# First batch of an attention and expert block: GpSimd's products to VectorE, its convolution adds to a tree of adding DMAs, and identity turns of TensorE moved ahead of the next batch's x

## The chip, the cores and the metric

One core of a Trainium2 chip runs the whole kernel. The metric is device time in microseconds, from the start to the end of one execution, as the median of several runs. Beside it stands one profiled execution, whose trace gives the start and the length of every instruction. The engines are TensorE (PE), VectorE (DVE), ScalarE (ACT), GpSimd (POOL) and SyncE (SP), which here only issues DMAs.

## The reference

The input is x of 4 batches, 1024 positions and 128 channels, float32. Two residual blocks follow each other; the first is the one that matters here.

```python
x = x + _layernorm(_L0_attn_ref(_layernorm(x), Wqkv, Wo, conv_w))
x = x + _layernorm(_L0_ffn_ref(_layernorm(x), gate_W, W1, b1, W2, b2, Ws1, bs1, Ws2, bs2, route_scale))

# inside the attention, 8 heads of 16 channels, offsets 0, 1, 2, 4, ... 512
sc = einsum('bhsd,bhskd->bhsk', qh, kg) / sqrt(d)      # q times k, k taken offset positions back
w = softmax(where(valid, sc, -inf))
tele = einsum('bhsk,bhskd->bhsd', w, vg)               # weighted v, offset positions back
conv = causal depthwise convolution of v with 7 taps
low = fq @ (fk.T @ v) / (fq . sum(fk) + 1e-6)          # fq, fk = elu + 1
return x + (tele + conv + low) @ Wo
```

The second block is a mixture of eight experts (two taken per position by a sigmoid gate) with a shared one. It starts one batch behind the attention, so that the first batch's attention runs alone.

## The kernel before

Everything is held in on-chip memory. A batch is 8 tiles of 128 positions (NT), two halves of 512 columns. The loop over b runs five times: in turn b the attention of batch b and the experts of batch b - 1 (units u0 and u1, its halves) are written into the same five instruction streams, one function for each engine. Each engine executes its stream in the order in which it stands; semaphores tie the streams together. Nothing reorders them, so a wait holds up all that stands behind it on its engine.

The attention of one batch goes like this. `product(eng, s, q)` (L283 is its multiply) multiplies qT with kT shifted by an offset, both channel-major, 1024 columns at a time (512 for the offset 512 and, in the first batch, in the first of three groups `s`). There are 4, 4 and 3 of them in the groups 0, 1 and 2; `sum_heads(b, s)` on TensorE (L1324) sums each head's channels into psA. A group's products lie in one of two sets of buffers, so that the third group waits for the sum of the first. Beside it VectorE makes the features fkT (L943) and fqT (L948), and TensorE makes the state kv (L1303), which VectorE masks (L974). After the third group the scores are copied by ScalarE, turned by TensorE, and VectorE does the softmax on them (`softmax_logits` from L982 on, `softmax_weights`), with the exponentials on ScalarE (L692). `weigh(b, j)` (L1026) then multiplies, tile by tile, the values v_tok and their shifted copies v_shift with the weights, into a ring of four buffers (TERM_BUFS); `sum_terms(b, j)` (L1353, L1356) on TensorE sums a tile's terms. Behind tile 4 stands `add_conv(b, 0)` (L1046), which adds the convolution's first half, and behind tile 7 `add_conv(b, 1)`. TensorE's sum of tile 4 and all behind it wait for the first of these, since the bank is used again. v_shift is made by 20-odd DMAs that SyncE issues as soon as v_tok is there.

The convolution is a sum of 7 taps. ScalarE scales each (`scale_first_taps`, L625: taps 0 to 3 behind fk_tok, taps 4 to 6 behind the scores) into buffers named by `first_tap(tap)`: convT, three tapT, gate_shared, x3T and hid. In the later batches six accumulating DMAs that GpSimd issues (`add_tap`, L495) sum them. In the first batch GpSimd itself does, by twelve adds of 512 columns (`first_conv`, L459), the first half ahead of the second. GpSimd also does three of the first batch's eleven products, those in POOL_PRODUCTS. Its stream in the first batch is: constants, the three products, gate_constants (three affine selects, L466), ln1 of the next batch (L489 to L492), the twelve adds, ln2 of the first half.

TensorE makes identity turns that nobody reads in three places of the first batch: WARM_UP at the start, FIRST_FILL_SUM (20) ahead of the third group's sum, FIRST_FILL_TERMS (24) behind the next batch's k and q projections and ahead of the first `sum_terms` (`keep_busy`, L1468). The next batch's x is normalised by ScalarE (`normalise1`, L598) behind the exponentials and when ln1 is done, and turned by TensorE (`turn_x`, L1252).

## Time and profile before

| | us |
|---|---|
| median of 3 runs | 300.31 (300.30 to 300.32) |
| the profiled execution, whole | 298.65 |
| its span, first to last instruction | 296.9 |
| busy in the span: TensorE, VectorE, ScalarE, GpSimd | 250.2, 245.5, 198.4, 110.9 |

The span is what the trace's times are counted in. The median lies 3.4 us above it. The page's chain of waits is the work that ended last, followed back from the end; a row of it says from when on and for how long the end waited for which operation. In a timeline row the numbers are start and length in microseconds, and the bracket tells how long the engine sat idle before it and which operation released it; where instructions are merged, the length is that of all. In a row by form the numbers behind the bar are busy time in microseconds, the mean in nanoseconds, and the idle time before. L numbers are lines of the kernel before.

### The profile page before, as it was taken

How to read it: one execution, taken by the hardware profiler on the slowest of the kernel's cores; microseconds unless marked ns; L12 is line 12 of the kernel's file. 1: busy time of each engine (PE TensorE's matmuls, PEld its weight loads, DVE VectorE, ACT ScalarE, POOL GpSimd, SP SyncE). 2: the span in 40 equal slices, each digit the busy share in tenths (PEclk: the TensorE clock that was granted, in tenths of full speed). 3: DMA queues.
4: the chain of work that ended last, by engine and by line, in shares of the span. 5: the costliest groups of instructions: out<-in, count | busy, mean ns of one | idle time of the engine just before them, and what ended most of it. 6: DMA issues, size and time to landing. Idle time of an engine off the chain costs nothing.

```text
span 296.9 us, 4788 instructions
## 1 busy us (share of the span) xinstructions
PE 250.2 (84%) x1639; PEld 173.5 (58%) x1639; DVE 245.5 (83%) x570; ACT 198.4 (67%) x461; POOL 110.9 (37%) x161
## 2 busy tenths in 40 slices
PE   5849909887699899989898899989898697699893
PEld 5424605776165467678546486777555485584383
DVE  6699989988997699799896899799957997727743
ACT  3476655447879956898499746989597253476841
POOL 5967699522434004025471104046530141230023
PEclk9998977999799999999999999999999999999999
DMA  7527602003989730308999601019899301000003
GB/s 202 129 78 216 195 0 72 2 0 62 235 244 202 172 71 0 108 0 164 253 236 234 127 9 38 0 27 226 265 218 217 71 3 35 0 3 1 0 13 95
DMA packets 22963, 31.34 MB, mean 106 GB/s; under 512 B 3909, under 2 KB 17054, under 8 KB 22938
## 3 DMA queue, kind: packets, MB, share of 16 engines
q1 hardware_dynamic: 20346, 21.59, 25.6%
q0 software_dynamic: 2592, 9.44, 17.5%
q8 instruction: 13, 0.21, 0.3%
q14 instruction: 12, 0.10, 0.1%
HBM read 5.07 MB, written 2.10 MB: 24 GB/s over the span
## 4 chain that ended last, share of the span: by engine, by line
PE 41%; DVE 31%; ACT 18%; issue 5%; POOL 4%; POOLq 0%; DVEq 0%; ACTq 0%
DVE prods L1026 7%; DVE prods L283 5%; PE psH L1356 5%; PE psY L1459 4%; PE psF L1421 3%; PE psG L1459 3%; PE psA L1459 3%; PE psA L1252 3%; DVE hid L1137 3%; PE psA L1324 2%; ACT xn L718 2%; PE psF L1396 2%; ACT xn L598 2%; DVE den L997 2%; PE psY L1303 2%
## 5 line engine op out<-in xcount | busy, mean ns | idle before, releaser
L474 POOL TENSOR_SCALAR var<-ss 128x4 f32<-128x4 f32 (+1 forms) x25 | 13.5, 539 | 105.8 <-ACT squares L764 51.6
L283 DVE TENSOR_TENSOR prods<-qT,kT 128x1024 f32<-128x1024 f32 (+1 forms) x44 | 50.9, 1212 | 2.2 <-ACT qT L587 2.2
L1356 PE MATMUL psH<-ident,prods 128*128 128x128 f32 x324 | 40.1, 273 | 0.0
L1356 PEld LDWEIGHTS psH<-ident,prods 128*128 128x128 f32 x324 | 36.4, 141 | 2.3 <-issue 2.3
L1026 DVE TENSOR_TENSOR prods<-v_shift,prob 128x896 f32<-128x896 f32 x32 | 35.7, 1115 | 0.0
L1137 DVE TENSOR_TENSOR hid<-hid,psG 128x512 f32<-128x512 f32 x32 | 20.8, 683 | 15.8 <-PE psG L1445 15.2
L476 POOL TENSOR_TENSOR rstd<-var,neg_half 128x4 f32<-128x4 f32 (+2 forms) x28 | 31.8, 1137 | 2.3
L1324 PE MATMUL psA<-prods,slot_sel 128*32 128x512 f32 x168 | 26.1, 677 | 6.1 <-DVE prods L283 5.9
L1421 PE MATMUL psF<-x3T,w 128*128 128x512 f32 x58 | 29.0, 610 | 0.4 <-ACT gexp L732 0.3
L1026 DVE TENSOR_TENSOR prods<-v_tok,prob 128x128 f32<-128x128 f32 (+2 forms) x60 | 25.5, 450 | 0.0
L495 POOL DMA_DIRECT2D convT<-tapT x9 | 8.2, 913 | 43.4 <-DMA convT<-tapT 24.6
L1260 PE MATMUL psA<-xnT,wqkv 128*128 128x512 f32 x36 | 18.6, 646 | 1.6 <-ACT xnT L587 1.6
L1459 PE MATMUL psY<-w,hid 128*128 128x128 f32 x140 | 16.6, 277 | 3.2 <-DVE prods L1010 3.2
L1459 PEld LDWEIGHTS psY<-w,hid 128*128 128x128 f32 x140 | 15.9, 192 | 5.7 <-DVE prods L1010 5.7
L740 ACT ACTIVATE hid<-psF,b1c 128x512 f32<-128x512 f32 x29 | 18.6, 682 | 0.7 <-PE psF L1421 0.5
L1421 PEld LDWEIGHTS psF<-x3T,w 128*128 128x128 f32 x58 | 9.7, 189 | 12.5 <-issue 8.5
L1468 PE MATMUL psG<-ident 128*128 128x128 f32 x100 | 14.0, 302 | 3.1 <-POOL ident L409 3.1
L1468 PEld LDWEIGHTS psG<-ident 128*128 128x128 f32 x100 | 13.1, 158 | 5.2 <-POOL ident L409 3.1
L1324 PEld LDWEIGHTS psA<-prods,slot_sel 128*32 128x32 f32 x168 | 5.5, 115 | 15.8 <-issue 13.5
L1353 PE MATMUL psH<-ident,prods 128*128 128x128 f32 x32 | 9.2, 288 | 6.2 <-DVE prods L1046 3.9
L764 ACT ACTIVATE squares<-psY 128x128 f32<-128x128 f32 x14 | 3.7, 277 | 14.8 <-PE psY L1459 14.8
L660 ACT ACTIVATE tapT<-vT,cw 128x1024 f32<-128x1024 f32 x12 | 13.1, 1137 | 0.0
(237 smaller groups left out, 612.1 us busy)
## 6 DMA issues: line engine op xcount, KB each, us to landing
v_shift<-v_tok SPq DMA_DIRECT2D x20, 448.0 KB
convT<-tapT POOLq DMA_DIRECT2D x9, 512.0 KB, 4.9
x_res<-L_attn_x SPq DMA_DIRECT2D x4, 512.0 KB, 9.6
out<-y_out SPq DMA_DIRECT2D x7, 256.0 KB, 2.3
x_in<-L_attn_x SPq DMA_DIRECT2D x3, 512.0 KB, 4.1
v_shift<-v_tok SPq DMA_DIRECT2D x4, 384.0 KB
tapT<-tapT POOLq DMA_DIRECT2D x3, 512.0 KB, 9.8
convT<-kexp POOLq DMA_DIRECT2D x3, 512.0 KB, 7.5
```

Source lines behind the costliest of these rows:

```text
L283: return eng.tensor_tensor(prods[:, QUADS * (s % 2) + q, t0:t1], qT[:, t0:t1], kT[:, PRE - off + t0:PRE - off + t1], ALU.mult)
L474: nc.gpsimd.tensor_scalar(var[:, cols], src, scale, EPS, ALU.mult, ALU.add).then_inc(step, 1)
L476: return nc.gpsimd.tensor_tensor(rstd[:, cols], var[:, cols], neg_half[:, cols], ALU.pow)
L740: nc.scalar.activation(hid[:, c, half_cols(u)], hidden_bank(u, c), ACT.Gelu, bias=b1c[:, c:c + 1]).then_inc(hidden_free, 1)
L1026: return nc.vector.tensor_tensor(dst, src.rearrange("p m (h d) -> p m h d", d=HD), w, ALU.mult)
L1137: nc.vector.tensor_tensor(hid[:, c, cols], hid[:, c, cols], psG[:, c % 2, :], ALU.mult).then_inc(gated, 1)
L1260: pe.matmul(psA[:, half, :], wqkv[:, bass.ts(part, P)], xnT[(b + 1) % 2][:, bass.ts(half, HALF)], start=True, stop=True).then_inc(psA_full, 1)
L1324: ins = pe.matmul(psA[32 * q:32 * q + 32, half, :], ksum_sel[:] if low else slot_sel[:, s, :], fqT[:, cols] if low else prods[:, QUADS * ( ...
L1356: ins = pe.matmul(dst, terms[:, j % TERM_BUFS, m, :], ident[:], is_transpose=True, start=False, stop=(m == live[-1]))
L1421: pe.matmul(hidden_bank(u, c), w1[:, bass.ts(c, P)], x3T[:, half_cols(u)], start=True, stop=True).then_inc(hidden_full, 1)
L1459: ins = pe.matmul(output_tile(u, n), hid[:, c, bass.ts(j, P)], w2[:, c, :], start=(c == CH - 1), stop=(c == CH - 2))
L1468: pe.transpose(bank[:, bass.ts(k % TPH, P)], ident[:], ident[:])
```

## The change

Three things, all in the first batch. First, POOL_PRODUCTS and `first_pool_products` go: VectorE does all eleven products. Second, `first_conv` goes: six accumulating DMAs of 512 KB, issued by GpSimd, sum the seven taps as a tree, 1 into 0, 3 into 2 and 5 into 4, then 2 into 0 and 6 into 4, then 4 into 0. The first three are issued ahead of ln1 of the next batch, the other three behind it; each waits for the taps and for the DMAs that it builds on. Both halves' `add_conv`, and the first tap of the next batch, wait for the last DMA. Third, 40 identity turns (FIRST_FILL_X) stand ahead of the next batch's `turn_x`, and FIRST_FILL_TERMS is 10 in place of 24.

GpSimd's stream before, from the last constants to the first adds (line numbers differ between the two kernels by a few; gate_sel is the constant of gate_constants, L489 to L492 are ln1):

```order
L442 MEMSET neg_half 1x1
L283 TENSOR_TENSOR prods<-qT,kT 128x1024 x3
L466 AFFINE_SELECT gate_sel<-gate_sel 24x512 x3
L470 MEMSET neg_half 1x1
L489 TENSOR_SCALAR neg_mean<-mv 128x8
L474 TENSOR_SCALAR var<-mv 128x8
L476 TENSOR_TENSOR rstd<-var,neg_half 128x8
L492 TENSOR_TENSOR nmr<-neg_mean,rstd 128x8
L459 TENSOR_TENSOR convT<-convT,tapT 128x512 x3
```

And the same place after the change:

```order
L442 MEMSET neg_half 1x1
L469 AFFINE_SELECT gate_sel<-gate_sel 24x512 x3
L473 MEMSET neg_half 1x1
L445 DMA convT<-tapT 128x1024
L445 DMA tapT<-tapT 128x1024
L445 DMA gate_shared<-x3T 128x1024
L492 TENSOR_SCALAR neg_mean<-mv 128x8
L477 TENSOR_SCALAR var<-mv 128x8
L479 TENSOR_TENSOR rstd<-var,neg_half 128x8
L495 TENSOR_TENSOR nmr<-neg_mean,rstd 128x8
L445 DMA convT<-tapT 128x1024
L445 DMA gate_shared<-hid 128x1024
```

The products and the adds are gone, the selects have moved up, and ln1 now stands behind the first three DMAs.

TensorE's stream before, from the turned scores to the first term sum:

```order
L1252 MATMUL psA<-ident,prods 128x128 x8
L1342 MATMUL psH<-kv,fqT 128x128 x4
L1342 MATMUL psY<-kv,fqT 128x128 x4
L1252 MATMUL psA<-ident,xn 128x128 x8
L1260 MATMUL psA<-xnT,wqkv 128x512 x4
L1468 MATMUL psG<-ident 128x128 x24
L1353 MATMUL psH<-ident,prods 128x128
```

And after:

```order
L1254 MATMUL psA<-ident,prods 128x128 x8
L1342 MATMUL psH<-kv,fqT 128x128 x4
L1342 MATMUL psY<-kv,fqT 128x128 x4
L1468 MATMUL psG<-ident 128x128 x40
L1254 MATMUL psA<-ident,xn 128x128 x8
L1262 MATMUL psA<-xnT,wqkv 128x512 x4
L1468 MATMUL psG<-ident 128x128 x10
L1353 MATMUL psH<-ident,prods 128x128
```

A row of 40 turns stands ahead of the turning of xn, and the row behind the projections is shorter by 14.

```diff
--- before.py
+++ after.py
@@ -47,8 +47,7 @@
 SLOTS, QUADS = 3, 4
 TERM_BUFS = 4
 WARM_UP = 20
-FIRST_FILL_SUM, FIRST_FILL_TERMS = 20, 24
-POOL_PRODUCTS = ((0, 3), (1, 3), (2, 2))
+FIRST_FILL_SUM, FIRST_FILL_X, FIRST_FILL_TERMS = 20, 40, 10
 FILL_SUM = 12
 FILL_FRONT = 5
 FILL_X3, FILL_C4, FILL_LOGITS = 10, 4, 8
@@ -243,7 +242,8 @@
         terms_ready, terms_summed = sem("terms_ready"), sem("terms_summed")
         tap_scaled, sums_added, side_added = sem("tap_scaled"), sem("sums_added"), sem("side_added")
         first_ld, first_xn = [sem(f"first_ld{h}") for h in range(2)], [sem(f"first_xn{h}") for h in range(2)]
-        first_turned, first_products, first_taps, first_added = sem("first_turned"), sem("first_products"), sem("first_taps"), sem("first_added")
+        first_turned, first_taps = sem("first_turned"), sem("first_taps")
+        first_pairs, first_sums = [sem(f"first_pair{i}") for i in range(3)], [sem(f"first_sum{i}") for i in range(3)]
         hT_ready, y_ready = sem("hT_ready"), sem("y_ready")
         ss2_ready, x2_ready, ss3_ready, xn3_ready = sem("ss2_ready"), sem("x2_ready"), sem("ss3_ready"), sem("xn3_ready")
         front_full, front_free = sem("front_full"), sem("front_free")
@@ -441,23 +441,26 @@
                     nc.gpsimd.memset(first_pref[:, :, e:e + 1], float(EXPERTS - e))
                 nc.gpsimd.memset(neg_half[0:1, 0:1], -0.5).then_inc(consts_ready, 1)
 
-            def first_pool_products():
-                pool.wait_ge(consts_ready, 2)
-                pool.wait_ge(psA_free, freed(-1, PSA_Q, 1))
-                for s, q in POOL_PRODUCTS:
-                    if s == 2:
-                        pool.wait_ge(group_summed, 1)
-                    product(nc.gpsimd, s, q).then_inc(first_products, 1)
-
-            def first_conv(half):
-
-                cols = bass.ts(half, HALF)
-                for tap in range(1, TAPS):
-                    pool.wait_ge(first_taps, tap + 1)
-                    if tap > 1:
-                        pool.wait_ge(first_added, (TAPS - 1) * half + tap - 1)
-                    nc.gpsimd.tensor_tensor(convT[0][:, cols], convT[0][:, cols], first_tap(tap)[:, cols],
-                                            ALU.add).then_inc(first_added, 1)
+            def add_first(into, tap, signal):
+                nc.gpsimd.dma_start(first_tap(into), first_tap(tap), accum_op=ALU.add).then_inc(signal, N_DMA)
+
+            def first_conv_pairs():
+                for pair in range(2):
+                    pool.wait_ge(first_taps, 2 * pair + 2)
+                    add_first(2 * pair, 2 * pair + 1, first_pairs[pair])
+                pool.wait_ge(first_taps, 6)
+                add_first(4, 5, first_pairs[2])
+
+            def first_conv_sums():
+                pool.wait_ge(first_pairs[0], N_DMA)
+                pool.wait_ge(first_pairs[1], N_DMA)
+                add_first(0, 2, first_sums[0])
+                pool.wait_ge(first_taps, TAPS)
+                pool.wait_ge(first_pairs[2], N_DMA)
+                add_first(4, 6, first_sums[1])
+                pool.wait_ge(first_sums[0], N_DMA)
+                pool.wait_ge(first_sums[1], N_DMA)
+                add_first(0, 4, first_sums[2])
 
             def gate_constants():
                 for part in range(3):
@@ -545,8 +548,8 @@
             first_rstds()
             constants()
             more_constants()
-            first_pool_products()
             gate_constants()
+            first_conv_pairs()
             for b in range(B + 1):
                 attn, ffn, more = b < B, b >= 1, b < B - 1
                 u0, u1 = 2 * b - 2, 2 * b - 1
@@ -566,8 +569,7 @@
                     ln4(u0)
                     add_residual(u0)
                 if b == 0:
-                    first_conv(0)
-                    first_conv(1)
+                    first_conv_sums()
                 if attn:
                     ln2(2 * b)
                 if more:
@@ -648,7 +650,7 @@
                     if tap == 0:
                         act.wait_ge(psA_free, freed(b - 1, PSA_V, 1))
                         if b == 1:
-                            act.wait_ge(first_added, 2 * (TAPS - 1))
+                            act.wait_ge(first_sums[2], N_DMA)
                         else:
                             act.wait_ge(hT_ready, upto(b - 1, 2, 0))
                     elif tap == 4:
@@ -955,7 +957,7 @@
                     dve.wait_ge(y_ready, upto(b, 2, 0))
                 if s == 2:
                     dve.wait_ge(group_summed, upto(b, 2, 1))
-                mine = [q for q in range(QUADS) if TERMS[SLOTS * q + s] != LOW and (b or (s, q) not in POOL_PRODUCTS)]
+                mine = [q for q in range(QUADS) if TERMS[SLOTS * q + s] != LOW]
                 if b == 0 and s == 0:
                     dve.wait_ge(psA_free, first_count(PSA_Q, 0))
                     for q in mine:
@@ -963,7 +965,7 @@
                     dve.wait_ge(psA_free, first_count(PSA_Q, 1))
                 for n, q in enumerate(mine):
                     ins = product(nc.vector, s, q, HALF if b == 0 and s == 0 else 0, T)
-                    ins.then_inc(prod_ready, 2 if b == 0 and q == mine[-1] else 1)
+                    ins.then_inc(prod_ready, 1)
                     beside(n)
 
             def linear_state(b, beside):
@@ -1041,7 +1043,7 @@
                 if b:
                     dve.wait_ge(sums_added, N_DMA * upto(b - 1, N_SUMS, N_SUMS))
                 else:
-                    dve.wait_ge(first_added, (TAPS - 1) * (half + 1))
+                    dve.wait_ge(first_sums[2], N_DMA)
                 cols = bass.ts(half, HALF)
                 nc.vector.tensor_tensor(hT[:, cols], psH[:], convT[b % 2][:, cols], ALU.add).then_inc(hT_ready, 1)
 
@@ -1306,8 +1308,6 @@
             def sum_heads(b, s):
 
                 pe.wait_ge(prod_ready, upto(b, N_PRODUCTS[2], N_PRODUCTS[s]))
-                if b == 0:
-                    pe.wait_ge(first_products, s + 1)
                 if s == 2:
                     pe.wait_ge(fq_ready, upto(b, 1, 1))
                     pe.wait_ge(kv_ready, upto(b, 1, 1))
@@ -1506,6 +1506,8 @@
                     if ffn:
                         turn_x3(u1)
                         gates_expert_major(u0)
+                    if b == 0:
+                        keep_busy(FIRST_FILL_X, psG[:, 1, :])
                     if more:
                         turn_x(b + 1)
                     if ffn:
```

## Rows read from the trace of the kernel before

**Rows 1.** Chain of waits: start us, us, what; first batch.

```profile
...
12.43 10.91 DVE prods L283 x9
...
31.53 0.18 DVE kv L974
...
36.24 0.13 DVE zden L982
...
46.64 7.85 DVE prods L1026 x7
...
59.81 0.61 DVE prods L1046
...
60.85 1.20 PE psH L1356 x11
...
69.07 0.70 DVE prods L1046
...
```

**Rows 2.** VectorE's groups by form, 75 to 240 us: shapes, busy us, mean ns, idle.

```profile
...
L283 DVE TENSOR_TENSOR prods<-qT,kT 128x1024 f32<-128x1024 f32 x27 | 31.5, 1213 | 0.0
L1026 DVE TENSOR_TENSOR prods<-v_shift,prob 128x896 f32<-128x896 f32 x19 | 20.6, 1083 | 0.0
...
L1026 DVE TENSOR_TENSOR prods<-v_tok,prob 128x128 f32<-128x128 f32 x22 | 6.3, 284 | 0.0
...
L283 DVE TENSOR_TENSOR prods<-qT,kT 128x512 f32<-128x512 f32 x3 | 2.0, 668 | 0.0
...
```

**Rows 3.** Groups by form, VectorE, 12 to 31 us.

```profile
...
L283 DVE TENSOR_TENSOR prods<-qT,kT 128x512 f32<-128x512 f32 x7 | 8.6, 1303 | 2.2 <-ACT qT L587 2.2
L283 DVE TENSOR_TENSOR prods<-qT,kT 128x1024 f32<-128x1024 f32 x4 | 5.6, 1445 | 0.0
...
```

**Rows 4.** Timeline, TensorE: start us, us, instructions, idle before and releaser.

```profile
...
29.30 2.35 PE L1468 MATMUL psG<-ident 128*128 128x128 f32 x20
...
44.03 1.30 PE L1252 MATMUL psA<-ident,xn 128*128 128x128 f32 x5 [7.09 <-ACT xn L598]
...
```

**Rows 5.** Timeline, ScalarE and GpSimd, 27 to 41 us.

```profile
...
27.24 3.24 ACT L625 ACTIVATE tapT<-vT,cw 128x1024 f32<-128x1024 f32 x3
...
34.04 0.20 POOL L489 TENSOR_SCALAR neg_mean<-mv 128x8 f32<-128x8 f32 x1 [2.39 <-DVE mv L921]
...
35.38 1.14 ACT L625 ACTIVATE x3T<-vT,cw 128x1024 f32<-128x1024 f32 x1
...
36.31 0.20 POOL L492 TENSOR_TENSOR nmr<-neg_mean,rstd 128x8 f32<-128x8 f32 x1
...
40.76 3.18 ACT L598 ACTIVATE xn<-x_in,nmr,rstd 128x128 f32<-128x128 f32 x8
...
```

**Rows 6.** Windows: PE, PEld, DVE, ACT, POOL busy, TensorE clock, DMA share, GB/s.

```profile
...
41.50:44.00 2.50, 0.00 (x0) 0.00 (x0) 2.43 (x3) 2.43 (x7) 2.27 (x2) 0.50 0.00 0
44.00:48.00 4.00, 3.97 (x11) 2.73 (x12) 3.93 (x6) 1.28 (x3) 3.80 (x3) 0.50 0.45 131
...
```

**Rows 7.** Accumulating DMAs: issues, landings at 71, 134, 103; windows; v_shift's queue.

```profile
...
70.37 1.11 POOL L495 DMA_DIRECT2D convT<-tapT  x1 [3.78 <-ACT tapT L660]
71.16 1.21 POOL L495 DMA_DIRECT2D tapT<-tapT  x1
...
convT<-tapT POOLq DMA_DIRECT2D x1, 512.0 KB, 4.8
tapT<-tapT POOLq DMA_DIRECT2D x1, 512.0 KB, 9.2
...
tapT<-tapT POOLq DMA_DIRECT2D x1, 512.0 KB, 11.0
...
convT<-tapT POOLq DMA_DIRECT2D x1, 512.0 KB, 4.5
...
104.00:108.00 4.00, 3.78 (x9) 1.52 (x10) 3.86 (x8) 2.98 (x5) 0.17 (x1) 1.00 0.69 131
...
q1 hardware_dynamic: 102, 0.27, 49.3%
...
```

## The prediction

> **What bounds the kernel now.** I read the chain of waits first, since it says whose work sets the end, and only its first 70 us, since the change touches nothing behind them. In the first batch the chain is VectorE's nearly all the way: it starts the products at 12.4 us, reads the turned scores at 36.24, starts to weigh the values at 46.64, adds the first half's convolution at 59.81 and the second half's at 69.07 [rows 1]. Next I ask which of these steps are as long as they have to be. The same operations have undisturbed durations in the later batches, where GpSimd adds and multiplies nothing: a product of 1024 columns 1213 ns, of 512 columns 668 ns, a v_shift term 1083 ns, a v_tok term of one tile 284 ns [rows 2]. In the first batch the same two products take 1445 and 1303 ns [rows 3]; the difference falls together with GpSimd's own three products and its adds. TensorE is the second reader: its identity fill of 2.35 us ends just as kv is ready (31.7), it then waits 7.09 us for the next batch's xn, and works on at half clock behind that [rows 4, 6]. ScalarE, GpSimd's order and the DMAs come last, because they are what the change leans on [rows 5, 7].
>
> **Part 1, products on VectorE.** VectorE gets nine products of 512 and six of 1024 columns instead of seven and four. The first two groups have nine of 512 and three of 1024: 9 x 0.668 + 3 x 1.213 = 9.7 us by the undisturbed durations (less by what overlaps between neighbours), against the 10.91 us that seven and two take now beside GpSimd [rows 1 to 3]. GpSimd's three affine selects of gate_sel, which ran behind its products, now run beside these; VectorE's last two products lay beside them at 1445 ns or so against 1213, so three selects may cost some 0.7 to 1.4 us. I take the keys' features 0.6 us earlier (bounds: 0.5 later to 1.5 earlier). Here TensorE takes over: it turns fk, sums the second group, makes kv's sum, and then has 20 identity turns of 2.35 us before the third sum. In the profile that fill is just covered by VectorE; now VectorE is earlier, so the fill is on the path, and the third sum comes only 0.6 to 0.7 us earlier. The turned scores are then complete at about 34.5, where VectorE, which comes from kv to zden in 4.5 us (31.7 to 36.24 [rows 1]), would be there at 33.7 and waits. So the softmax starts at 34.5 for 36.24: **1.7 us**.
>
> **Part 2, no adds on GpSimd.** The twelve adds of 512 columns go. They run beside the softmax and the first tiles. VectorE weighs tiles 0 to 4 in 59.81 - 46.64 = 13.2 us. The same fourteen terms undisturbed are 5 x 1.083 + 6 x 0.284 + three of two or three tiles, each under 0.6 (at most 384 of a v_shift term's 896 columns): 8.2 to 8.9 us [rows 1, 2]. With the softmax's own multiply undisturbed as well, weighing would start at 44.0 and reach the first convolution add at 51.7 to 52.9.
>
> **Part 3, the 40 turns.** They fill the 7.09 us of TensorE's wait. 20 turns take 2.35 us in the profile [rows 4], so 40 take 4.7: from about 36.2 to 40.9, before xn is there (42.4, below), so they delay nothing. TensorE's clock stands at 0.50, its 1.2 GHz level, from the end of that wait until 48 [rows 6]; kept at 2.4 GHz the turns of xn and the four projections no longer lag, and with 10 turns for 24 the first term sum can start at about 48.4 (ScalarE empties xnT, kT and qT in six steps from 43.0 on). A tile's sum is 11 turns in 1.20 us [rows 1], four tiles of 9 to 11 turns under 4.6: TensorE has tiles 0 to 3 at 52.9. So by the engines alone the first add would come at **52.9**, 6.9 us early.
>
> **Part 4, ln1 behind three DMAs.** GpSimd computes neg_mean to nmr of the next batch from 34.04 to 36.51 [rows 5]; the change puts the wait for tap 5 ahead of it. ScalarE writes tap 5 (x3T) from 35.38 to 36.5 [rows 5], 0.7 earlier with the scores: 35.8. An issue of 0.8 us and ln1's 2.5 us follow: 39.2. ScalarE's xn waits for that, but also for its own exponentials, behind which it starts at 40.76 now [rows 5] and at 39.1 then. A tie: it costs 0.1 to 0.2, xn is done at 42.4.
>
> **Part 5, the tree of DMAs.** It is new work for the DMA engines, and the convolution add of VectorE waits for its root. Six accumulating DMAs of 512 KB, three levels deep, on one queue. The rows: such a DMA with nothing beside it lands 4.5 us after its issue, of which its data keep the DMA engines busy for 0.69 of 4 us, about 2.8 us; of two issued 0.8 us apart beside v_shift's traffic the first lands after 4.8, the second after 9.2, which is 71.16 + 9.2 - 70.37 - 4.8 = 5.2 us behind the first; a second one at 134 us landed after 11.0 [rows 7]. Here v_shift runs until 36 (the last 49% slice [rows 7]) and, with two accumulations beside it, until about 41, still ahead of its reader at 45. The sum: tap 1 is written at 28.3 [rows 5], now 27.9; first pair lands after some 7 (between 4.8 and the pair's shared 9.2): 34.9; second 5.2 behind it: 40.1; third, issued at 35.9, 3.8 behind it (between 2.8 and 5.2, since v_shift ends there): 43.9; the add of 2 into 0, queued at 40.2, shares the DMA engines with the next x load, 4.0: 47.9; the add of 6 into 4, issued at 44.0, 2.8 behind it: 50.7; only then the last, 4.5: **55.2**. VectorE adds at 55.3 or 55.4. Bounds: with 4.8 for the first and 2.8 for each queued one (the third is issued at 35.9 and takes 4.5) the root lands at about 50.5; with 11.0 - 4.8 = 6.2 or 5.2 for each it lands at 62. Both ends are kept. I take 55.4 since both kinds of rows, shared and alone, occur on its way.
>
> The Trainium skill ("DMA: Bandwidth & Descriptors", the SWDGE path) gives about 2.0 us plus bytes / 436 GB/s for a DMA issued by GpSimd, 3.2 us here and 1.2 for a queued one; the profile's rows have 4.5 and 2.8 [rows 7], so accumulation is dearer than that fit. By the fit the tree would be done before 50 and the add would come at 52.9.
>
> **Behind the add** nothing is changed: from the first convolution add to the second 69.07 - 59.81 = 9.3 us, mostly TensorE (tile 4's sum, the output, the projection of v, three sums). But TensorE now sits idle from 52.9 until 56.1, and the profile shows what it does after idle: 0.50 behind the 7.09 us wait [rows 4, 6]. With a shorter wait it may fall or not; if it does, some 2.4 us of turns at 1.2 GHz cost 1.2 us. I count it.
>
> **The sum.** First add 59.7 -> 55.4: -4.3; clock +1.2: -3.1. Against the profiled execution: span 296.9 -> 293.8. The median of the runs stands 3.4 above that span (300.31), with the same distance 297.2.
>
> **Rivals.** (A) *The tree is no bound*: it lands before 52.9, VectorE never waits, the whole 6.8 us come: 293.5. For it: 2.8 us of data per DMA, and half of the tree behind v_shift's traffic. Against: depth three with 4.5 at its end, one queue. (B) *The tree lands later than GpSimd's adds did*. With 5.2 for every queued one and 6 for the second, as when v_shift or x traffic is beside all of them, the root is at 61 to 62; VectorE, TensorE and the next batch stand behind the add; TensorE is idle for over 8 us and starts at 1.2 GHz for 3 to 4 us of work, +1.7. The time is 300.3 + (61.3 - 59.7) + 1.7 = 303.6. It decides at a root at 58.0: from there on the saving no longer pays for the clock. For it: both ends of the rows reach it, and nothing in the profile shows an accumulation issued beside another queue's backlog of this size in the first batch. (C) *They cancel*: root at 57.7 to 58.3, 300.3. (D) *The change does not do what it says*: VectorE's products were not slowed by GpSimd but by something in batch 0 alone, so the scores come 0.5 late, the terms stay slow and the first add comes at about 59: within 0.5 us of now. Rows 2 against 3 speak against it, since only what lies beside GpSimd's work is slow.
>
> **How the numbers follow.** Tree as bound, add between 53.6 and 57.7 (forecast 297.2, its own range 295.2 to 299.5): 0.52. A: 0.20. B: 0.17. C and D: 0.11, of which about 0.08 within 0.2% (0.6 us, about what a measurement of this kernel can tell from no change), the rest a little faster or slower. Faster 0.73, same 0.08, slower 0.19. The range reaches from A's time less half a us, 293.0, to 301.5, which leaves out the worse half of B and little below: about 0.1 each side.
>
> **What would show it.** In the changed profile: products of 512 and 1024 columns near 668 and 1213 ns but for the three selects; kv and the scores under 1 us earlier, zden at 34.5 behind TensorE; ln1's nmr near 39.2 and xn done at 42.4; clock 1.00 through 41 to 48; v_shift terms at 1083 ns; VectorE idle ahead of its first convolution add for 2 to 4 us, released by a DMA, at 55.4; a stretch of 0.50 behind it; 9.3 to 10.5 us to the second add. It is wrong if VectorE does not wait there (A), if it waits until after 58 (B), if v_shift lands after 45, or if a later batch loses what the first gains.

## The result, and the profile after

The changed kernel takes 297.75 us at the median (295.9 to 300.19, 17 runs), the kernel before 300.31 beside it. The ratio is 0.992 with a 95% interval of 0.9901 to 0.9938: 2.4 us faster, 1.9 to 3.0. The forecast was 297.2. Its profiled execution has a span of 295.5 us, for 296.9 before, which is only 1.4. Executions of one and the same kernel here spread over 4 us (298.87 to 303.25 before), and the longer ones mostly have the lower mean granted clock of TensorE (in the changed kernel 0.957 at 300.19 and 0.984 at 295.9, though 0.979 at 299.81). So a comparison of two traces tells where time is spent, and the ratios and medians tell how much. The ratios leave out executions over 1.5% above the same kernel's shortest; the medians beside them are of all. The profiled execution of before took 298.65, below the shortest of the 17 beside it (298.87). So the pair of traces accounts for 1.4 us of the 2.4 to 2.6, and no kept trace shows where the rest lies.

The chain of waits of the changed kernel, the steps of its first batch (start us, us, what), which answer to [rows 1]:

```profile
...
12.52 10.34 DVE prods L283 x12
...
31.74 2.18 PE psG L1468 x20
...
40.28 2.28 POOL rstd L479
...
42.87 3.19 ACT xn L600 x8
...
58.28 0.70 DVE prods L1048
...
67.64 0.70 DVE prods L1048
...
```

The chain that was VectorE's has become TensorE's, GpSimd's and ScalarE's: through the fill of 20 turns, through ln1's power behind the third DMA, through xn, and then on TensorE to the first convolution add (the projections and tiles are left out of the lines above). That add is at 58.28 for 59.73, 1.45 us earlier; the second at 67.64 for 69.07, 1.43 earlier, and nothing of this is lost later (1.4 at the end). So the whole gain of this execution stands at the first add, and 9.36 us lie between the adds as before.

VectorE's groups by form from 12 to 31 us, to be read against [rows 3], and from 43 to 67 us against [rows 2]:

```profile
...
L283 DVE TENSOR_TENSOR prods<-qT,kT 128x1024 f32<-128x1024 f32 x6 | 7.0, 1215 | 0.0
L283 DVE TENSOR_TENSOR prods<-qT,kT 128x512 f32<-128x512 f32 x9 | 6.9, 840 | 2.2 <-ACT qT L589 2.2
...
```

```profile
...
L1028 DVE TENSOR_TENSOR prods<-v_shift,prob 128x896 f32<-128x896 f32 x8 | 8.7, 1085 | 0.0
L1028 DVE TENSOR_TENSOR prods<-v_tok,prob 128x128 f32<-128x128 f32 x9 | 2.5, 285 | 0.0
...
```

VectorE works undisturbed now, except for the products of 512 columns that lie beside the three selects: 840 ns for 668, 1.5 us over nine. But VectorE no longer decides. Its timeline from 31 to 59 us has the waits:

```profile
...
31.77 0.29 DVE L976 TENSOR_TENSOR kv<-psY,head_mask 128x128 f32<-128x128 f32 x1 [3.08 <-PE psY L1305]
...
37.26 0.23 DVE L984 TENSOR_SCALAR zden<-psA 128x64 f32<-128x64 f32 x1 [0.67 <-PE psA L1254]
...
58.28 0.69 DVE L1048 TENSOR_TENSOR prods<-psH,convT 128x512 f32<-128x512 f32 x1 [1.73 <-PE psH L1356]
...
```

kv is no earlier than before (31.77 for 31.44), and VectorE reads the turned scores 1.1 us later (37.26 for 36.16). On TensorE they are complete 2.0 us later, at 37.1 for 35.1; before, VectorE came to them last. The windows of the same trace (busy time of PE, PEld, DVE, ACT, POOL, then TensorE's granted clock, DMA share, GB/s) show why:

```profile
...
20.00:22.00 2.00, 1.97 (x12) 0.24 (x4) 2.00 (x3) 0.57 (x1) 0.00 (x0) 0.50 0.85 245
22.00:24.00 2.00, 0.00 (x0) 0.00 (x0) 2.00 (x4) 0.00 (x0) 0.00 (x0) 0.50 0.85 253
24.00:29.00 5.00, 4.94 (x22) 2.16 (x22) 4.70 (x6) 3.53 (x5) 0.00 (x0) 0.50 0.77 234
...
47.00:50.00 3.00, 2.87 (x5) 1.18 (x4) 3.00 (x7) 1.39 (x3) 0.00 (x0) 0.50 1.07 179
...
```

TensorE runs at 0.50, its 1.2 GHz level, from 19.7 to 29.9 us. It had been idle from 16.5 to 18.95, summed the first group, and was idle again from 22 to 24 for the keys' features. The turns of fk, the second group and kv's sum, which took from 24.5 to 29.3 before, take from 24.1 to 31.6. The turns of fk, before and after:

```profile
...
24.54 1.09 PE L1252 MATMUL psF<-ident,fkT 128*128 128x128 f32 x8 [0.67 <-DVE fkT L943]
...
```

```profile
...
24.06 1.97 PE L1254 MATMUL psF<-ident,fkT 128*128 128x128 f32 x8 [2.09 <-DVE fkT L945]
...
```

How long the clock is down here differs between executions. Five kernels of the experiments below (products only, no tree, ln1 first, and the two with the root on VectorE and no early fills) give TensorE the same work up to this place. In their traces the clock is up until 24 to 25 us and down only from there to about 28; kv is ready at 30.6 to 30.9 and zden starts at 36.1 to 36.4. The old fills have it as here (31.87 and 37.35). So some 1 us of what is late in this trace is this execution's, and two traces are fairly compared only when their clocks fall in the same places.

A second such place lies in the next batch. From the second convolution add of the first batch to the first one of the second batch it is 51.4 us in the traces of before, changed, products only, no tree, early fills, ln1 first and the two last kernels, where the clock is back by about 79 us. It is 52.8 to 53.1 in old fills, early fills and a hold, fills only, tree only and the root alone, and 54.3 in the one without the fill of 20, where it is down later, beside more of TensorE's work. The same windows of the changed kernel, then of the old fills:

```profile
...
75.00:78.00 3.00, 2.59 (x14) 0.22 (x4) 2.96 (x19) 2.96 (x10) 2.60 (x5) 0.56 0.88 211
81.00:84.00 3.00, 3.00 (x30) 2.12 (x31) 3.00 (x8) 1.47 (x3) 0.00 (x0) 1.00 0.80 252
...
```

```profile
...
75.00:78.00 3.00, 1.92 (x16) 0.42 (x16) 3.00 (x8) 3.00 (x17) 1.45 (x2) 1.00 1.09 214
81.00:84.00 3.00, 2.47 (x5) 1.43 (x6) 3.00 (x6) 0.84 (x2) 0.00 (x0) 0.53 0.78 241
...
```

These 1.4 to 2.9 us are in the times of the experiments and not in their first batch. Most executions of the kernel before are 1.6 us longer than its profiled one, which this place could explain; it isn't shown, since only one trace of each kernel is kept.

The tree, by GpSimd's issues and the time from issue to landing, in us:

| DMA | issued | takes | landed |
|---|---|---|---|
| 1 into 0 | 29.06 | 6.8 | 35.9 |
| 3 into 2 | 31.13 | 10.5 | 41.6 |
| 5 into 4 | 38.80 | 5.4 | 44.2 |
| 2 into 0 | 43.12 | 4.8 | 47.9 |
| 6 into 4 | 44.76 | 6.9 | 51.7 |
| 4 into 0, the root | 52.16 | 4.5 | 56.7 |

```profile
...
52.16 0.85 POOL L445 DMA_DIRECT2D convT<-gate_shared  x1 [6.54 <-DMA gate_shared<-hid]
...
```

```profile
...
convT<-gate_shared POOLq DMA_DIRECT2D x1, 512.0 KB, 4.5
...
```

In this execution the tree is done 1.6 us before TensorE is.

### The profile page after: what moved, and what is told of

It is laid out like the page before. It is cut to its first block, busy times and chain, and to the rows that moved or that the text cites. A ratio compares the mean times of both kernels' runs of the same rounds, so it can differ in the third digit from the quotient of the medians.

```text
span 295.5 us, 4824 instructions
## 1 busy us (share of the span) xinstructions
PE 253.9 (86%) x1665; PEld 175.9 (60%) x1665; DVE 236.4 (80%) x574; ACT 198.6 (67%) x461; POOL 88.3 (30%) x152
## 4 chain that ended last, share of the span: by engine, by line
PE 49%; DVE 20%; ACT 20%; POOL 5%; issue 5%; POOLq 0%; DVEq 0%; ACTq 0%
PE psH L1356 6%; PE psA L1324 4%; PE psY L1459 4%; PE psA L1262 4%; DVE prods L283 3%; PE psF L1421 3%; DVE prods L1028 3%; ACT xn L600 3%; PE psG L1459 3%; PE psA L1459 3%; PE psA L1254 3%; DVE hid L1139 3%; PE psY L1305 3%; POOL rstd L479 2%; ACT xn L720 2%
## 5 line engine op out<-in xcount | busy, mean ns | idle before, releaser
L1356 PEld LDWEIGHTS psH<-ident,prods 128*128 128x128 f32 x324 | 36.4, 141 | 2.3 <-issue 2.3
L1028 DVE TENSOR_TENSOR prods<-v_shift,prob 128x896 f32<-128x896 f32 x32 | 34.7, 1083 | 0.0
L479 POOL TENSOR_TENSOR rstd<-var,neg_half 128x4 f32<-128x4 f32 (+2 forms) x28 | 32.5, 1160 | 2.3
L1324 PE MATMUL psA<-prods,slot_sel 128*32 128x512 f32 x168 | 27.4, 705 | 4.2 <-DVE prods L283 4.2
L1028 DVE TENSOR_TENSOR prods<-v_tok,prob 128x128 f32<-128x128 f32 (+2 forms) x60 | 20.8, 373 | 2.1 <-PE psH L1356 2.1
L1468 PE MATMUL psG<-ident 128*128 128x128 f32 x126 | 16.4, 289 | 3.1 <-POOL ident L409 3.1
L1468 PEld LDWEIGHTS psG<-ident 128*128 128x128 f32 x126 | 15.5, 150 | 5.2 <-POOL ident L409 3.1
L1324 PEld LDWEIGHTS psA<-prods,slot_sel 128*32 128x32 f32 x168 | 5.5, 118 | 14.5 <-issue 12.2
```

The source lines that it names most:

```text
L479: return nc.gpsimd.tensor_tensor(rstd[:, cols], var[:, cols], neg_half[:, cols], ALU.pow)
L1028: return nc.vector.tensor_tensor(dst, src.rearrange("p m (h d) -> p m h d", d=HD), w, ALU.mult)
L1324: ins = pe.matmul(psA[32 * q:32 * q + 32, half, :], ksum_sel[:] if low else slot_sel[:, s, :], fqT[:, cols] if low else prods[:, QUADS * ( ...
L1356: ins = pe.matmul(dst, terms[:, j % TERM_BUFS, m, :], ident[:], is_transpose=True, start=False, stop=(m == live[-1]))
L1468: pe.transpose(bank[:, bass.ts(k % TPH, P)], ident[:], ident[:])
```

## First experiments: the three parts alone

The experiments come in three groups; each kernel ran beside the kernel before on the same chip. The first four take the change apart.

**Products only.** GpSimd's three products go to VectorE, nothing else.

```diff
-POOL_PRODUCTS = ((0, 3), (1, 3), (2, 2))
+POOL_PRODUCTS = ()
...
-            first_pool_products()
...
-                if b == 0:
-                    pe.wait_ge(first_products, s + 1)
```

> Of the three parts only the first: VectorE makes all eleven products of the first batch; GpSimd's adds and TensorE's fills stand as in the kernel before. Theory P (what bounds the first batch after the change is TensorE up to the scores, at 1.2 GHz from 19.7 to 29.9 us, so faster products gain nothing there): kv at 31 to 32 us as before, scores not earlier, the time within 0.6 us of the kernel before (300.3), rather 0.3 to 1 slower since the fill of 20 turns is no longer covered. Rival Q (VectorE's products were the gain): 1.5 to 2.5 us faster, 298 to 299.

Measured: ratio 0.994, interval 0.991 to 0.9969, median 299.15 against 300.35. Theory P's range for the time is missed, and Q's nearly met, though the trace is nearer to P: kv is 0.75 us earlier (30.69), zden is where it was, and the first convolution add is 0.2 us earlier than before, the second too (68.87):

```profile
...
36.17 0.23 DVE L981 TENSOR_SCALAR zden<-psA 128x64 f32<-128x64 f32 x1 [0.67 <-PE psA L1251]
...
59.52 0.68 DVE L1045 TENSOR_TENSOR prods<-psH,convT 128x512 f32<-128x512 f32 x1
...
```

The two traces are 0.2 us apart in their spans too (296.7 for 296.9), the medians 1.2, the ratio 1.8 and the means of all executions only 0.6 (299.92 for 300.55). The rest lies in how the executions are spread, which a single trace doesn't show. It stays open whether the products alone gain anything.

**Fills only.**

```diff
-FIRST_FILL_SUM, FIRST_FILL_TERMS = 20, 24
+FIRST_FILL_SUM, FIRST_FILL_X, FIRST_FILL_TERMS = 20, 40, 10
...
+                    if b == 0:
+                        keep_busy(FIRST_FILL_X, psG[:, 1, :])
```

> Only the third part: 40 identity turns ahead of the next batch's x and 10 in place of 24 behind it. Theory P: the term sums of TensorE start 2 to 3 us earlier (50.5 for 53.3) but VectorE, slowed by GpSimd's adds, comes to its first convolution add at nearly the same time, so at most the 0.95 us that it stands ahead of tile 3 is gained: 299.3 to 300.3. Rival Q (the clock of TensorE behind its wait was the bound): 2 us or more faster, under 298.3.

Measured: ratio 1.0095, interval 1.0056 to 1.0134, median 304.04. A miss for both theories: the fills alone make the kernel 2.9 us slower. The trace (TensorE's timeline, then windows) shows how:

```profile
...
55.54 0.33 PE L1353 MATMUL psH<-ident,prods 128*128 128x128 f32 x1 [2.24 <-DVE prods L1026]
...
61.64 0.45 PE L1353 MATMUL psH<-ident,prods 128*128 128x128 f32 x1 [0.87 <-DVE prods L1046]
61.88 2.55 PE L1356 MATMUL psH<-ident,prods 128*128 128x128 f32 x11
...
```

```profile
...
53.00:57.00 4.00, 1.73 (x14) 1.25 (x12) 4.00 (x5) 1.71 (x2) 3.42 (x2) 1.00 0.00 0
57.50:61.00 3.50, 2.61 (x11) 2.21 (x11) 2.47 (x5) 0.00 (x0) 0.00 (x0) 0.50 0.00 0
61.00:67.00 6.00, 5.36 (x25) 5.39 (x26) 5.51 (x10) 0.00 (x0) 0.00 (x0) 0.50 0.00 0
...
```

With 10 turns for 24 TensorE comes to the term sums at 51 us, and VectorE, which GpSimd's adds slow, can't feed it: it is busy 1.73 of 4 us, the clock falls to 1.2 GHz at 57.3, and the eleven turns of a tile take 2.55 us for 1.36. The first add is at 60.81, the second 12.2 us behind it at 72.98, for 9.3; of the 5.3 us by which the span is longer, 3.9 stand there and 1.4 in the next batch. TensorE, early at a slow feeder, lost its clock here. That it need not is seen in the trace of the kernel without the tree, below.

**Tree only.** The tree stands in place of `first_conv`, GpSimd keeps its products, the fills are the old ones.

```diff
-                    first_conv(0)
-                    first_conv(1)
+                    first_conv_sums()
...
-                    dve.wait_ge(first_added, (TAPS - 1) * (half + 1))
+                    dve.wait_ge(first_sums[2], N_DMA)
```

> Only the second part: the tree of DMAs in place of GpSimd's twelve adds; GpSimd keeps its three products, the fills are as before. Theory P: scores at 36.2 as before or a little later (ln1 stands behind tap 5, so xn is later by 2 us), v_shift terms at 1.08 us, VectorE's first convolution add at 58 to 59 behind TensorE, not behind a DMA: 0.5 to 1.5 us faster, 298.8 to 299.8. Rival R (the tree is the bound): VectorE waits for a DMA ahead of that add, 300 or more.

Measured: ratio 0.9961, interval 0.9935 to 0.9987, median 299.37; P's range, 1.2 us faster. VectorE's timeline has the first add released by TensorE, so R falls; it is 1.25 us earlier than before, and 1.7 us are lost again in the next batch:

```profile
...
58.48 0.69 DVE L1058 TENSOR_TENSOR prods<-psH,convT 128x512 f32<-128x512 f32 x1 [1.73 <-PE psH L1368]
...
```

**No tree.** The changed kernel with `first_conv` back: products on VectorE, new fills, GpSimd's adds.

```diff
-                    first_conv_sums()
+                    first_conv(0)
+                    first_conv(1)
```

> Products on VectorE and the fills as in the changed kernel, but GpSimd's twelve adds in place of the tree. Theory P: the scores come 1 us later than before (the fill on TensorE's path), the terms are slowed by the adds again (v_shift and v_tok terms with means above 1.1 and 0.4 us), the first convolution add at 60 to 61: 300.3 to 301.5, so that the whole gain of the change hangs on the tree. Rival Q: under 299.

Measured: ratio 1.0012, interval 0.9972 to 1.0051, median 301.27: no gain without the tree, Q falls. The adds slow the terms as before (groups by form, 43 to 67 us; with the tree they are 1085 and 285 ns):

```profile
...
L1017 DVE TENSOR_TENSOR prods<-v_shift,prob 128x896 f32<-128x896 f32 x8 | 9.7, 1212 | 0.0
L1017 DVE TENSOR_TENSOR prods<-v_tok,prob 128x128 f32<-128x128 f32 x9 | 5.1, 580 | 0.0
...
```

Its profiled execution is one of its shortest, 298.39, and has the first add at 59.50, earlier than P said. TensorE has the same early start and the same gaps there as in fills only, and keeps its clock:

```profile
...
53.00:57.00 4.00, 1.73 (x16) 1.49 (x15) 4.00 (x6) 2.55 (x3) 2.07 (x2) 1.00 0.00 0
57.50:61.00 3.50, 2.44 (x21) 1.99 (x19) 3.50 (x8) 0.00 (x0) 0.00 (x0) 1.00 0.00 0
...
```

So the same busy time went before a fall in one trace and before none in the other. That the longer executions of this kernel (up to 303.64) are those with a fall is likely, and not shown.

The parts alone come to -0.6%, +0.95% and -0.4%, together about nothing; the whole is -0.8%. So they are not additive. The fills cost beside GpSimd's adds (0.95% here, and 0.7% from products only to no tree) and pay beside the tree (1.1% from the old fills, below, to the changed kernel). What tree and fills give with GpSimd's products kept wasn't run.

## Second group: what bounds the changed kernel

**The old fills.** The changed kernel with no turns ahead of xn and 24 behind the projections.

```diff
-FIRST_FILL_SUM, FIRST_FILL_X, FIRST_FILL_TERMS = 20, 40, 10
+FIRST_FILL_SUM, FIRST_FILL_X, FIRST_FILL_TERMS = 20, 0, 24
```

> The changed kernel with the fills of the kernel before: none ahead of the next batch's x, 24 behind its k and q projections. Theory P (the parts are worth something only together: the fills need the tree, since TensorE then reaches the term sums first and VectorE, no longer slowed by GpSimd's adds, keeps it busy): TensorE idles about 7 us ahead of xn, its projections at 1.2 GHz and 24 turns put the first term sum at 55 to 56, the first convolution add at 59.5 to 60.5: 1 to 2.5 us slower than the changed kernel, 298.8 to 300.3. Rival Q (the fills are worth nothing or harm, as they do alone): the same as the changed kernel or faster, 297.8 or less.

Measured: ratio 1.0028, interval 1.0001 to 1.0055, median 300.65: 2.9 us above the changed kernel. Direction and trace as P said, a little more than its range. TensorE's turns of xn follow an idle of 7 us, and 24 turns in place of 10 put the sums later; the first add is at 60.13 for 58.28, with the same clock ahead of the scores in both traces. That is 1.85 us of the 3.3 between the spans; the other 1.5 stand in the next batch, where the clock is down later:

```profile
...
52.84 2.78 PE L1468 MATMUL psG<-ident 128*128 128x128 f32 x24
...
```

```profile
...
60.13 0.69 DVE L1048 TENSOR_TENSOR prods<-psH,convT 128x512 f32<-128x512 f32 x1 [1.73 <-PE psH L1356]
...
```

**ln1 first.** Only the third DMA moves behind ln1.

```diff
-                pool.wait_ge(first_taps, 6)
-                add_first(4, 5, first_pairs[2])
...
             def first_conv_sums():
+                pool.wait_ge(first_taps, 6)
+                add_first(4, 5, first_pairs[2])
```

> The changed kernel with only the third DMA (tap 5 into tap 4) moved behind ln1 of the next batch on GpSimd. Theory P (behind the softmax the chain runs through tap 5, that issue, ln1 and xn to TensorE, and the tree has 1.6 us to spare at its root): nmr at 37 us for 42.8, xn starts behind the exponentials at 41.9 for 42.9, the first convolution add 0.7 to 1.2 us earlier: 296.6 to 297.1 by the median. Rival R (the tree's root is the bound, or right behind it): the third DMA is issued at 38.8 as before, nothing moves by more than 0.5 us.

Measured: ratio 0.9912, interval 0.9877 to 0.9948, median 298.28: no difference from the changed kernel that can be told, so P's gain in time is missed. In its trace ln1's last step is at 35.69, 7 us earlier, and TensorE has tiles 0 to 3 at 54.7 for 58.2. Of these 3.5 us, 1.0 is in the scores already (zden at 36.26) and 1.4 in the projections (3.80 us for 5.23), both by this execution's clock; the edit's own part is about 1.1, the wait of 0.96 for nmr that is gone. VectorE stands and waits for the tree's root:

```profile
...
57.41 0.69 DVE L1048 TENSOR_TENSOR prods<-psH,convT 128x512 f32<-128x512 f32 x1 [4.07 <-DMA convT<-gate_shared]
68.42 0.69 DVE L1048 TENSOR_TENSOR prods<-psH,convT 128x512 f32<-128x512 f32 x1 [1.85 <-PE psH L1356]
...
```

The first add gains 0.9 us, and then 11.0 us lie between the adds for 9.4, since TensorE has idled and its clock is down from 58.2 to 61.7. The two bounds, TensorE and the tree, lie 1.6 us apart in the changed kernel's trace, and in this one the clock takes back what was gained.

**No fill ahead of the third sum.**

```diff
-FIRST_FILL_SUM, FIRST_FILL_X, FIRST_FILL_TERMS = 20, 40, 10
+FIRST_FILL_SUM, FIRST_FILL_X, FIRST_FILL_TERMS = 0, 40, 10
```

> The changed kernel without the 20 identity turns ahead of the third group's sum. Theory P (that fill is on the path, 31.57 to 33.9 us in the trace of the changed kernel, where VectorE's kv is ready at 31.8): the scores and the zden step come 1.5 to 2.1 us earlier (VectorE's weight centring is then the bound at 36.4 to 36.6, so zden at 36.5 for 37.3: 0.7 us only on VectorE), xn 0.9 to 1.2 us earlier through tap 5, the first add about 1 us earlier: 296.5 to 297.2. Rival S (the fill holds the clock up): 1.2 GHz in the scores and their turning, no gain or up to 1 us slower.

Measured: ratio 1.001, interval 0.9976 to 1.0045, median 300.84: slower than the changed kernel by some 3 us, beyond what S said. Its profiled execution starts the products 1.4 us later than the others, at 13.88, behind GpSimd's last constant; counted from there, zden (at 36.67) is 0.8 us earlier than in the five traces with the same clock, which bears out P's path. But the add again waits for the root, at 58.24, and the second one follows 11.0 us later, in part at 1.2 GHz; a further 2.9 us are lost in the next batch. S's reason isn't seen: the clock is 1.00 through the scores and their turning (30 to 41 us). The profiled execution is its longest (302.04), and why most of the others are over 300 stays open.

**Early fills.** 18 turns ahead of the first group's sum, 24 behind it.

```diff
                         token_major_v(b)
                         pe.wait_ge(consts_ready, 1)
+                        keep_busy(18, psG[:, 1, :])
                     sum_heads(b, 0)
+                    if b == 0:
+                        keep_busy(24, psG[:, 1, :])
```

> The changed kernel with 18 identity turns ahead of the first group's sum and 24 behind it, in the stretches where TensorE waits for VectorE (16.5 to 18.9 and 22 to 24 us). Theory P (what was lost against the forecast is TensorE's clock, at 1.2 GHz from 19.7 to 29.9): the clock stays at 2.4 GHz, kv at 28.9 to 29.4 for 31.8, zden at 34.6 for 37.3, the first convolution add at 55.5 to 56.5: 1.8 to 2.8 us faster than the changed kernel, 295 to 296. Rival T (the turns only take TensorE's time, or the tree becomes the bound at 56.5): 0.5 us or less.

Measured: ratio 1.0004, interval 0.9963 to 1.0045, median 301.2. The time is T's and worse, the trace (298.57, one of its short executions) is P's up to the softmax. Here the clock is up from 16 to 44 us, and the turned scores are there when the forecast had them (34.5):

```profile
...
16.00:24.00 8.00, 7.13 (x62) 5.21 (x61) 8.00 (x11) 4.52 (x6) 0.56 (x2) 1.00 0.38 106
24.00:30.00 6.00, 5.98 (x50) 4.37 (x51) 5.67 (x11) 5.25 (x6) 1.11 (x1) 1.00 0.76 234
...
58.50:61.50 3.00, 2.60 (x13) 2.63 (x14) 3.00 (x7) 0.00 (x0) 0.00 (x0) 0.50 0.00 0
...
```

```profile
...
28.98 0.29 DVE L976 TENSOR_TENSOR kv<-psY,head_mask 128x128 f32<-128x128 f32 x1 [0.33 <-PE psY L1305]
...
34.47 0.23 DVE L984 TENSOR_SCALAR zden<-psA 128x64 f32<-128x64 f32 x1 [0.67 <-PE psA L1254]
...
58.07 0.69 DVE L1048 TENSOR_TENSOR prods<-psH,convT 128x512 f32<-128x512 f32 x1 [4.09 <-DMA convT<-gate_shared]
68.76 0.69 DVE L1048 TENSOR_TENSOR prods<-psH,convT 128x512 f32<-128x512 f32 x1 [1.85 <-PE psH L1356]
...
```

2.8 us gained at the scores, 0.2 left at the first add, 1.1 us lost at the second. With TensorE as fast as I had forecast, the tree is the bound; its root lands at 58.0, not at 55.2. The trace is 1.1 us longer than the changed kernel's; why the median is 3.5 us longer it doesn't show.

## Third group: the tree's depth and the clock behind it

**Early fills and a hold.** 28 more turns where TensorE waits for the first add.

```diff
                         sum_terms(b, j)
+                        if b == 0 and j == TPH - 1:
+                            keep_busy(28, psG[:, 1, :])
```

> The changed kernel with the 18 and 24 early turns and 28 more behind the sum of tile 3, where TensorE waits 3.2 us for VectorE's first convolution add and then works at 1.2 GHz. Theory P (the distance between the two convolution adds is 10.7 us there for 9.4 only because of TensorE's clock): first add at 58.1 behind the tree as without them, second add 9.3 to 9.5 behind it, 1.2 us faster than with the early turns alone in executions of the same kind. Rival V (the distance has another cause, the DMAs or ScalarE): still 10.5 or more.

Measured: ratio 0.9974, interval 0.9937 to 1.0012, median 299.68, 1.5 us below the early fills alone, though the intervals overlap. The add still waits for the root, and the second one is now 9.64 us behind the first for 10.69, with the clock at 1.00 in every window from 55 to 67. V falls; the clock is 1.05 us of that distance. (In the next batch this trace loses 1.45 us again.)

```profile
...
57.33 0.69 DVE L1048 TENSOR_TENSOR prods<-psH,convT 128x512 f32<-128x512 f32 x1 [3.44 <-DMA convT<-gate_shared]
66.97 0.69 DVE L1048 TENSOR_TENSOR prods<-psH,convT 128x512 f32<-128x512 f32 x1 [1.51 <-PE psH L1356]
...
```

**The root on VectorE.** The sixth DMA goes; VectorE adds the tree's two halves itself when they have landed, just ahead of the first convolution add, where it stood idle.

```diff
-                add_first(0, 4, first_sums[2])
...
+            def add_root():
+                dve.wait_ge(first_sums[0], N_DMA)
+                dve.wait_ge(first_sums[1], N_DMA)
+                nc.vector.tensor_tensor(first_tap(0), first_tap(0), first_tap(4), ALU.add).then_inc(first_rooted, 1)
...
                         if j == TPH:
+                            if b == 0:
+                                add_root()
                             add_conv(b, 0)
```

> The changed kernel with the tree's last level on VectorE: one add of 1024 columns (1.2 us) when the two DMAs under it have landed, ahead of the first convolution add, in place of the sixth DMA. Theory P (in the changed kernel's trace TensorE's sums end at 58.25 and the root lands at 56.7, in other executions the root is the later one): VectorE's add lies in its idle time, the first convolution add stays at 58.3 in an execution with the clock as in that trace and comes earlier in the others: 0.3 to 1.5 us faster than the changed kernel, 296.3 to 297.5. Rival R (the root is always hidden): the same within 0.3, 297.5 to 298.

Measured: ratio 0.9874, interval 0.9825 to 0.9923; but the median of all its executions is 297.83 (293.29 to 300.36) and their mean 297.96, for 297.75 and 297.86 of the changed kernel. So a gain of the root by itself isn't shown, which is nearer to R than to P. In its trace the first add is at 57.13, behind TensorE, and 1.15 us earlier than in the changed kernel's because the scores are (zden at 36.35).

**The root and ln1 first.** Both edits together.

> The same with ln1 of the next batch ahead of the third DMA too. Theory P (both bounds are then gone: TensorE's sums of tiles 0 to 3 end at 54.8, the second level of the tree lands at 52.3, and TensorE does not fall to 1.2 GHz behind the add): first convolution add at 55 to 56, 9.3 us to the second: 2 to 3.5 us faster than the changed kernel, 294.3 to 295.8. Rival R (the DMAs themselves were late, not the depth of the tree): the add behind a DMA at 57 or later, 296.5 to 298.

Measured: ratio 0.9872, interval 0.9823 to 0.9922, median 296.11 (6 runs), the span of its trace 293.6. P in direction, short of its size, and the interval overlaps that of the changed kernel. The first add is at 56.37, again behind TensorE, whose clock was down from 45.1 to 48.6 under the projections; 9.35 us to the second.

**The root, ln1 first and the early fills.**

> The same with 18 and 24 identity turns around the first group's sum as well. Theory P: kv at 29.0, zden at 34.5, TensorE's sums end at 52 to 53, the second level of the tree lands at 51 to 53 and is the bound: first add at 53 to 54.5; 0 to 1.5 us faster than without the turns, 293.5 to 295.5. Rival U (turns beside VectorE's work cost what they give): slower than without them.

Measured: ratio 0.9798, interval 0.9751 to 0.9845, median 294.88 (292.48 to 296.95, 6 runs): faster than both kernels, 5.5 us under the one before and 2.9 under the changed one, within P's range. Its trace, span 290.5:

```profile
...
51.96 1.23 DVE L1042 TENSOR_TENSOR convT<-convT,gate_shared 128x1024 f32<-128x1024 f32 x1 [0.42 <-DMA gate_shared<-hid]
53.29 0.69 DVE L1051 TENSOR_TENSOR prods<-psH,convT 128x512 f32<-128x512 f32 x1
62.65 0.69 DVE L1051 TENSOR_TENSOR prods<-psH,convT 128x512 f32<-128x512 f32 x1 [1.23 <-PE psH L1361]
...
```

VectorE, TensorE and the DMAs arrive together, TensorE's clock stays up from 16 to 69 us, and the first add is at 53.3, where part 3 of the prediction had put it for the engines alone (52.9). The same early turns that cost the changed kernel some 2.5 us by the ratios gain 1.2 by the medians here (2.2 by the ratios), since what they used to run into is gone. By the trace, a sixth DMA behind the landing at 51.9 would have put the root at about 57 (0.5 to its issue and 4.5 to land; an estimate), so VectorE's own 1.23 us add is what lets the gain through; ln1 first and early fills without it weren't run.

## Why the prediction was right, and where it wasn't

The time, the sign and the range held; the way there did so only in part. The bound that was given the largest chance, the tree at the first add, is not the bound in the profiled execution, and that the sum came within 0.6 us is in part luck, as the last point shows.

- *Undisturbed VectorE* (parts 1 and 2): as forecast, 1215, 1085 and 285 ns for 1213, 1083 and 284. The three selects cost the nine products of 512 columns beside them 1.5 us, for 0.7 to 1.4. Weighing began at 46.9 and not at 44.0, for the next two reasons.
- *The scores* (part 1): forecast complete at 34.5, read by VectorE at 37.26 here and at 36.1 to 36.4 in the five traces with the shorter stretch of low clock. This is the step that failed. I reckoned TensorE's fk turns, sums and state at the speed they had in the trace of before. There its clock was back at 2.4 GHz at 24.4, ahead of them; after the change it was down beside them, until 29.9 here and until about 28 in the five. kv itself came 0.6 to 0.8 us earlier in the five (30.6 to 30.9 for 31.44), as forecast, but from TensorE and not from VectorE, which waited 1.9 us for it. I had asked what an idle stretch of TensorE costs only for those behind xn and behind the add, not for the two before. With early fills, which keep the clock up, VectorE has the scores at 34.47, so the whole of the miss goes with the clock.
- *The fill of 20 turns on the path*: as forecast, 2.2 us of the chain. Taking it away gained nothing in time.
- *ln1 behind tap 5* was a tie in the forecast. It cost ScalarE a wait of 0.96 us, of which 0.64 are the power, 2.28 us for 1.64. With ln1 first the wait is gone and, as worked out there, TensorE comes some 1.1 us earlier.
- *The 40 turns*: a miss in detail. The projections ran at 1.2 GHz for 3.4 us nevertheless (the window from 47 to 50); TensorE had been idle for 2.8 us behind the turns, since xn came at 46.1 and not at 42.4. The fills as a whole are worth 2.9 us beside the tree by the medians (the run with the old fills), 1.85 of it seen at the first add.
- *The tree*: landings of 35.9, 41.6, 44.2, 47.9, 51.7 and 56.7 for the forecast's 34.9, 40.1, 43.9, 47.9, 50.7 and 55.2. The first pair was issued 1.2 us later than reckoned, at 29.06 for 27.9, since the taps wait for fk. The first took 6.8 us for some 7 and the root 4.5 as reckoned; from one landing to the next it was 5.7, 2.6, 3.7 and 3.8 for the forecast's 5.2, 3.8, 4.0 and 2.8. What was left out is 0.5 us from a landing to the issue that waits for it (44.2 to 44.76, 51.7 to 52.16). With early fills v_shift's DMAs released VectorE's first term only at 44.84, behind a wait of 0.66 us, where they were forecast to be done at about 41.
- *The bound at the first add*: forecast the tree at 55.4, found TensorE at 58.25 with the tree 1.6 us ahead. Rival A's "the tree is no bound" was true in this execution, but because TensorE was late and not because the tree was fast. The change of bound is shown by the runs with ln1 first and with early fills, where TensorE comes earlier and the same tree then holds VectorE for 4.1 us.
- *The clock behind the add*: 1.2 us forecast, nothing found, since TensorE wasn't idle there. Where it is idle the cost is 1.3 to 1.65 us (10.69 and 11.01 for 9.36), and 1.05 of 1.33 goes with the hold.
- *The sum*: -4.3 + 1.2 = -3.1 against -1.45 + 0 in the trace. That the median fell by 2.6 has a second part: I took the distance of 3.4 us between span and median as fixed. It isn't. The end of a profiled execution lies 1.8 to 2 us above its span (298.65 - 296.9, 297.46 - 295.5), and the rest was that the profiled execution was a short one, 298.65 where most take 300.3. So two errors, a gain too large by 1.65 us and a distance taken for a constant that was 2.25 and not 3.4, partly cancelled. That is luck, and no merit of the mechanism.

The Trainium skill ("DMA: Bandwidth & Descriptors", the SWDGE path) has a fit for a DMA issued by GpSimd, by which the prediction's estimate had the tree done before 50 us. The trace disagrees: the root alone takes 4.5 us, for 3.2 by the fit, and lands at 56.7.

## What to carry to other kernels

Before an engine is given its input earlier, ask what its clock will be there: work that is pulled forward can leave gaps elsewhere, and behind a gap TensorE may work at half its clock (here 1.3 us more behind the first add). A part that loses alone can pay beside another, as the fills did, so take a change apart before it is kept or dropped, and put it together again with the bound that it uncovered removed. In a tree of DMAs count the levels, each a whole landing plus 0.5 us to the next issue here, and try giving the last level to the engine that waits for it. And before two traces are compared, look where the clock is down in each: the same instructions had it down from 19.7 to 29.9 us in one execution and from 24 to 28 in another.

## What the runs showed that I had not expected

In fills only TensorE's clock fell behind 4 us in which it was busy for 1.73, with a longest wait of 2.24 us (the windows and rows above); in no tree it was busy for 1.73 of the same 4 us, waited 2.27, and the clock stayed up. GpSimd's power on 128x8 takes 1.64 to 1.67 us in some places and 2.25 to 2.28 in others, with the same operands; what makes the difference wasn't tried. The three affine selects take 4.85 us beside products of 1024 columns and 2.79 beside those of 512. And the executions of one kernel that has nothing random in it lie up to 7 us apart (the root on VectorE: 293.29 to 300.36), which makes single traces weak evidence for differences below 1%.
